# Two attention layers on one core: the third score bank goes over to the projection jobs ten units earlier, and two query projections move by a step

## The reference

```
x = x + tanh(g_xattn[0]) * xattn0(layernorm(x), ctx)   # 16 heads of 8,  256 queries, 512 keys
x = x + tanh(g_ffn[0])   * ffn0(layernorm(x))          # Hadamard, 4-bit activations, ternary weight
x = x + tanh(g_xattn[1]) * xattn1(layernorm(x), ctx)   # 16 heads of 64, 256 queries, 512 keys
x = x + tanh(g_ffn[1])   * moe(layernorm(x))           # 32 experts, top 4, and a shared one
```

## Time and profile before

| | |
|---|---|
| median of the runs | 269.39 us (269.26 to 269.96) |
| the profiled execution | 269.09 us, of which the span of its profile is 267.4 us |
| busy share of the span | TensorE 94%, VectorE 79%, ScalarE 71%, GpSimd 68% |
| granted TensorE clock | 0.999 |
| last scores of layer 1 (unit 63), first of layer 2 (unit 64) | 84.25 us, 85.21 us |

### The profile page before, as it was taken

One profiled execution on the slowest core, in us unless ns is written; L12 is line 12 of the kernel. 1 busy time (PEld: TensorE's weight loads), 2 busy tenths in 40 slices (PEclk: granted clock), 3 DMA queues, 4 the chain that ended last, 5 costly groups with the idle time before them and its releaser, 6 DMA issues. The chain is left out here.

```text
span 267.4 us, 6701 instructions
## 1 busy us (share of the span) xinstructions
PE 250.7 (94%) x1899; PEld 198.0 (74%) x1899; DVE 211.4 (79%) x657; ACT 188.8 (71%) x451; POOL 181.0 (68%) x272
## 2 busy tenths in 40 slices
PE   7888999998889999989999999999989999989994
PEld 4565667775656778768777788877767768979993
DVE  3999989999989896799677887777798624995673
ACT  2588879997899776847776676678776654555562
POOL 5667999885789675746743585348848795964380
PEclk9999999999999999999999999999999999999999
DMA  6648263200035754644574766766442051212530
GB/s 179 216 126 320 101 197 110 92 0 4 1 73 128 166 125 98 135 92 106 146 209 101 194 160 185 187 168 169 115 114 61 6 158 39 77 44 69 178 96 20
DMA packets 25475, 31.86 MB, mean 119 GB/s; under 512 B 4000, under 2 KB 18144, under 8 KB 25312
## 3 DMA queue, kind: packets, MB, share of 16 engines
q1 hardware_dynamic: 25008, 31.23, 43.5%
q10 hardware_dynamic: 432, 0.22, 0.3%
HBM read 14.32 MB, written 2.42 MB: 63 GB/s over the span
## 5 line engine op out<-in xcount | busy, mean ns | idle before, releaser
L631 POOL TENSOR_SCALAR probs<-probs,rsum 128x512 f32<-128x512 f32 x128 | 87.8, 692 | 52.4 <-DVE rsum L987 51.4
L774 ACT ACTIVATE probs<-masked,neg_max 128x512 f32<-128x512 f32 x128 | 91.7, 718 | 12.0 <-DVE neg_max L978 9.0
L1310 PE MATMUL bank<-ident,probs 128*128 128x128 f32 x512 | 78.5, 276 | 2.5 <-DVE probsT L995 1.2
L1310 PEld LDWEIGHTS bank<-ident,probs 128*128 128x128 f32 x512 | 58.6, 141 | 19.0 <-issue 10.7
L978 DVE CUSTOM_DVE_ANT_0 masked<-bank,mask 128x512 f32<-128x512 f32 x64 | 43.8, 685 | 15.3 <-PE bank L1446 14.7
L783 ACT ACTIVATE probsT<-bank 128x512 f32<-128x512 f32 x74 | 43.5, 588 | 16.0 <-PE bank L1310 15.6
L1483 PE MATMUL bank<-probsT,val 128*32 128x256 f32 (+1 forms) x512 | 46.6, 384 | 0.0
L995 DVE COPY probsT<-bank 128x512 f32<-128x512 f32 x54 | 36.8, 681 | 8.8 <-PE bank L1310 8.5
L978 DVE CUSTOM_DVE_ANT_0 masked<-bank,shared 128x512 f32<-128x512 f32 x64 | 43.3, 678 | 0.1
L1483 PEld LDWEIGHTS bank<-probsT,val 128*32 128x32 f32 (+1 forms) x512 | 24.4, 123 | 17.7 <-issue 4.8
L1439 PE MATMUL bank<-parts 128*128 128x512 f32 x64 | 31.1, 486 | 1.6 <-DVE neg_max L978 1.3
(11 more groups left out here) (257 smaller groups left out, 516.6 us busy)
## 6 DMA issues: line engine op xcount, KB each, us to landing
k_both<-k_low SPq DMA_DIRECT2D x32, 128.0 KB, 2.8
k_both<-k_high SPq DMA_DIRECT2D x32, 128.0 KB, 2.6
q<-q_split SPq DMA_DIRECT2D x32, 128.0 KB, 2.4
probsT<-staged_gate SPq DMA_DIRECT2D x32, 128.0 KB, 3.0
q<-q_split SPq DMA_DIRECT2D x32, 64.0 KB, 2.1
parts<-staged_k SPq DMA_DIRECT2D x7, 256.0 KB, 2.8
w_flat<-in_w SPq DMA_DIRECT2D x1, 1536.0 KB, 7.8
staged_q<-q_split SPq DMA_DIRECT2D x4, 256.0 KB, 2.6
```

What stands on the lines that cost most here:

```text
L631: pool.tensor_scalar(p, p, rsum[:, u % NCOL:u % NCOL + 1], 1.0, ALU.mult, ALU.mult).then_inc(normed, 1)
L774: act.activation(probs[:, u % NP, :], masked[:, u % NS, :], ACT.Exp, scale=-1.0, bias=neg_max[:, c:c + 1], accum_out=sums[:, c:c + 1]).the ...
L1310: ins = pe.transpose(dst[0:rows, t * P:t * P + P], src, ident[:, :])
```

## The change

The second job bank joins at step 52 and not 60; so that it can, layer 1's scores use three banks only up to unit 53 and two from unit 54. The query job of a block in layer 2 goes 11 steps ahead of its block, except block 9's, which stays at 12. Only `q8` moves by this in effect: from step 52 to 53 (blocks from 10 on had 11 already). The job that first takes the second bank waits for the last unit that used it.

```
-TWO_BANKS_AT = 60
+TWO_BANKS_AT = 52
+THREE_BANKS_UNTIL = 54
...
-        plan.setdefault(k.first - early - (12 if k.m < 10 else 11), []).append(("q", k.m))
+        plan.setdefault(k.first - early - (11 if k.m != 9 else 12), []).append(("q", k.m))
...
 def score_home(u):
 
-    return u % 3 if u < L1_AT else (u + 1) % 2
+    return u % 3 if u < THREE_BANKS_UNTIL else u % 2
...
                 if j == SECOND_BANK:
-                    pe.wait_ge(maxed, L1_AT - 1)
+                    pe.wait_ge(maxed, THREE_BANKS_UNTIL)
```

## The result

The changed kernel takes 270.65 us (22 runs, 269.88 to 271.21) beside 269.76 us for the kernel before (22 runs in turn with it): a ratio of 1.0027, 95% interval 1.0017 to 1.0037. It is slower by 0.7 us (0.5 to 1.0). The ratio is not the quotient of the two medians, which lie 0.89 us apart, inside the same interval. The profiled execution took 270.20 us with a span of 268.5; that of before 269.09 and 267.4.

What follows compares the result with a forecast made beforehand. TensorE was taken to set the pace from `scores(64)` on, whose start waits for `q8`'s landing. +0.43 (bank) and +0.60 (order) gave +1.0 us: 270.1 profiled, 270.4 us median, 0.4% slower; range 269.0 to 271.4.

Steps and rivals of the forecast that it cites:

- the one chain that the prediction followed: Layer border: bank turned, `x_low`, `q8`, its two parts, four issues, landing, which sets when `scores(64)` starts; 1.03 us late.
- Two banks, 0.43 us: At unit 56: `scores(56)` waits for `mask_max(54)`, not `mask_max(53)`, making `x_low` and `q8`'s low part 0.43 us late.
- Unit 63 at 84.5: `scores(63)` waits for `mask_max(61)` until about 84.5, against 84.25: 0.25 us, ahead of a `scores(64)` that waits anyway.
- The query a step later, 0.60 us: On VectorE `copy_turned(52)` and `mask_max(59)` now precede `q8`'s low part, making it 0.60 us later by order.
- The stalls that went, at nothing: TensorE's waits ahead of `q8` (0.68 us) and `q9` (0.43 us) go, costed at nothing; `turn(53)` stays behind GpSimd's `norm(53)`.
- over 1 us of idle ahead of `scores(64)`: Sign expected in the profile after: `scores(64)` at 86.2 with over 1 us of TensorE idle ahead of it.
- The delay passes whole: From `scores(64)` on TensorE sets the pace without a real pause, so the +1.0 us reaches the end undiminished.
- The sum: Whole kernel: +0.43 and +0.60, that is +1.0 us on the profiled 269.09, so 270.1; median 270.4 us.
- same: Outcome for the kernel's time: no change distinguishable, within about 0.3% or 0.8 us; chance 0.33.
- slower: Outcome for the kernel's time: slower by more than about 0.3% or 0.8 us; chance 0.54.
- the range: Kernel time expected 8 times in 10: 269.0 to 271.4 us.
- The clock rival: The granted clock falls for a stretch like 85 to 90 us, matmuls taking twice as long: some 274 us; chance 0.02.

Runs made afterwards that it cites:

- score banks alone: Kernel before with two score banks from unit 54, all jobs as before (`TWO_BANKS_AT = 60`, `q8` at step 52): 1.0011 against before.
- third bank kept to unit 56: Changed kernel with the third score bank given up at unit 57 and not 54, all else as changed: 1.0022 against before.
- split wait: `scores(64)` and `scores(65)` wait only for `q8`'s two transfers that stack head 0: 0.9999 in the changed kernel, 0.9980 in the kernel before, both against before.
- twelve waits: Twelve already met waits in SyncE's program ahead of `k8`'s stacking: 1.0003, again 0.9999, in the changed kernel; 0.9984 in the kernel before; all against before.
- first four experiments: Bank part alone, query part alone, third score bank until unit 56, and split wait in the changed kernel: 1.0008, 1.0009, 1.0022, 0.9999 against before.
- `k10` alone in the second bank: Kernel before with split wait, twelve waits and second job bank from step 58, not 60; third score bank kept to unit 62: 0.9966 against before, median 269.12 us.
- bank part alone: Changed kernel with `q8` left at step 52; two score banks from unit 54, second job bank from step 52: 1.0008 against before.
- query part alone: Kernel before with `q8` at step 53, score and job banks as before: 1.0009 against before.
- best of the parts: Changed kernel with third score bank until unit 56, `q8` at step 52 and the split wait; second job bank from step 52: 0.9979 against before.

## Why the prediction was right, and where its size was off

**Direction and mechanism: right.** Slower, through the one chain that the prediction followed. Each stage of the table above is met within 0.02 us up to `scores(64)`, and the splitting of one wait takes the loss away and leaves all the earlier waits in place.

**Two banks, 0.43 us: right.** Shown at `x_low` and the low part by the score banks alone (0.44 late) and by the third bank kept to unit 56 (`x_low` back at 78.47). In the changed kernel the other tightened units cost nothing: `scores(63)` waits 0.67 us, at 84.53 against 84.25 before, ahead of a landing that is later still.

**Unit 63 at 84.5: right by luck.** The prediction put `mask_max(61)` at its time before, 83.89, though it had just made VectorE 0.43 us late. It came at 83.78 because the idle 0.61 us ahead of `q8`'s low part was filled, which takes back more than the 0.43. With `q8` left at step 52 that idle time stays, `mask_max(61)` is at 84.3 and `scores(63)` at 85.07 to 85.09, and there this wait is as late as the landing.

**The query a step later, 0.60 us: right in size.** The part alone moves the low part by 0.58. TensorE's wait of 0.68 us ahead of `q8` was no loss but slack ahead of a later wait: it went, and the time did not fall.

**The stalls that went, at nothing: right.** `turn(53)` is at 80.10 on the scale of before, behind GpSimd's norm as said. One sign was off: the prediction wanted over 1 us of idle ahead of `scores(64)`, and the trace has 0.76, because the wait at `scores(63)` had put `turn(57)` 0.29 us later as well.

**The delay passes whole: not quite, and this is the term that was mis-sized.** The sum had +1.0 us at the end. The profiles give 1.01 at `scores(64)` but 0.87 at the mix right behind and at `turn(58)`, and 1.1 - 0.28 = 0.8 at the end of the span. The prediction costed the second bank at nothing for `k10`, with the words that TensorE issues without a pause from 85.21. There was a short pause: `k10` at 85.77 waited for `q9`'s low part, whose row begins at 85.25. The lines of before are:

```profile
85.77 0.50 PE L1315 MATMUL bank<-ctx_parts,w_early 128*128 128x512 f32 x1
86.10 0.40 PE L1316 MATMUL bank<-ctx_parts,w_early 128*128 128x512 f32 x1
```

With its own bank, it starts 0.54 us behind `scores(64)` and not 0.56, and its second matmul follows after 0.23 us and not 0.33. That is 0.12 to 0.14 back.

**Against the runs, 0.7 and not 1.0 us.** The 0.13 is one part. What is left, 0.87 against 0.7, needs no cause of its own: the interval is 0.5 to 1.0 us, and the medians lie 0.89 apart. There may be one all the same. Both profiled executions were quicker than a typical one, that of before (269.09 us) by 0.67 and that of the changed kernel (270.20) by 0.45. In the profile of before the second issue of `q8` was not stretched. In all six other profiles with `q8` at step 52 it was, by 0.13 to 0.86 us; in the four with all parts of the change, where the issue comes 1.0 us later, never. So a typical run of before may start `scores(64)` later than its profile shows, and have less left to lose. That the split wait and the twelve waits, each put into the kernel before, measured faster than their profiles (0.9980, 0.9984) speaks for it; the distribution itself was not measured, so this is argued and not shown. The record has a rival to it that no run separates. Ten of the 35 runs of before that stand beside the first four experiments have a mean granted clock of 0.996 to 0.998, and their median is 270.06 us beside 269.70 for the rest; with `k10` alone in the second bank six of twelve have 0.997, and 269.35 beside 268.72. How many such runs a kernel has thus moves its median too.

**The chances.** The measured 0.27% lies just under the 0.3% that parts "same" from "slower", where I had 0.33 and 0.54, and inside the range; the interval leaves out a change of nothing. The clock rival did not come: the granted clock is 1.00 in all windows of the changed kernel, the level of 2.4 GHz, with 4.25 of 5.00 us busy in one, and none of its 22 runs has a mean under 0.998. So the warning of the Trainium skill, "TensorE: Matmul & The Clock Gate", section "A second HAM failure mode: psum-queue depth-cycling", finds no case in pauses of this size.

## What to carry to other kernels

When a stall on the busiest engine is filled, look for what the stalled work was early for: if it feeds a transfer, the time of its result counts and not the time of the engine. Follow the late chain to the first instruction that it truly gates, and split the wait there by what is read first; here this one split was worth the whole change. A score bank given up earlier than its job needs it is a wait with nothing bought. Only `k10` had a use for the second bank: given it at step 58, with three score banks kept, the mix is 0.40 us ahead of before; given it with the third score bank gone from unit 57, 0.02 behind (both with the split wait).

## What the runs showed of the hardware

Two things lengthened SyncE's issues, neither of them in the kernel's own text.

- **A hole at a place of the program.** In all nine profiles without the twelve waits the third issue starts 0.41 to 0.43 us behind the end of the second. In the four with them it is 0.03 to 0.04 us, and the hole, 0.42 to 0.44 us long, stands between the first two issues of `k8` instead. An 8 KB transfer of an instruction queue, which starts at 83.0 to 84.8 us in the nine, starts at 78.6 to 78.9 us in the four. So the hole is bound to a place in SyncE's instructions. What fills it stays open: that transfer starts 0.6 to 0.9 us after the hole has ended, so the hole is no wait for its data.
- **An issue held by an instruction transfer.** A 16 KB transfer of the other instruction queue starts at 80.3 to 82.0 us in every profile and takes 0.93 to 1.56 us. Where it ends late, the second issue is held and ends 0.38 to 0.40 us after it:

```
                               16 KB transfer ends    second issue: length, end
bank part alone                      82.95                 1.07   83.34
query part alone                     82.78                 0.81   83.18
third bank until unit 56             82.92                 0.87   83.30
split wait, before                   82.08                 1.17   82.47
best of the parts                    81.81                 0.92   82.20
score banks alone                    83.07                 0.74   83.45
twelve waits, before                 81.87                 0.90   82.25
k10 to the second bank               82.68                 1.47   83.07
before                               81.33                 0.61   81.95
changed kernel                       82.37                 0.61   83.23
```

The numbers are those of each profile's own span. In the last two, and in the three others that are not listed, the transfer ended over 0.5 us ahead of the issue's own end, and the issue has its 0.61 us. The same is seen away from `q8`: in the two profiles of before and of the changed kernel nine more lengthened issues, from 95 to 191 us, end 0.25 to 0.45 us after such a transfer, and three do not. The Trainium skill, "Runtime: NRT & Kernel Launch", section "Instruction fetch mechanics", says that an engine's instructions are refilled in 16 KiB blocks while it runs and that crossing such a block is mostly hidden. The traces here bear out transfers of 16 KB; beside one of them an issue is not hidden but up to 0.86 us longer, and in a chain with no slack that is lost. No run shows whether the hole is a refill.
